# Gather sums in three steps, projection chunk by chunk: one change to a time-mix and mixture-of-experts kernel

## Time and profile before

| | us |
|---|---|
| median of 3 runs | 392.32 |
| the profiled execution | 395.08 |
| its span | 393.3 |
| PE busy | 322.4 (82% of the span) |
| DVE busy | 269.1 (68%) |
| POOL busy | 207.5 (53%) |
| ACT busy | 158.8 (40%) |
| projection matmuls L623 | 95.7, 744 instructions |
| all four periods, first pair to last product | 97.7 to 356.5 |
| tail: last projection, 16 gathers, sums, stores | 356.5 to 393.3 |

### The profile page before, as it was taken

One profiled execution on the slowest core, in us unless ns is written; L12 is line 12 of the kernel. 1 busy time (PEld: TensorE's weight loads), 2 busy tenths in 40 slices (PEclk: granted clock), 3 DMA queues, 4 the chain that ended last, 5 costly groups with the idle time before them and its releaser, 6 DMA issues.

```text
span 393.3 us, 6787 instructions
## 1 busy us (share of the span) xinstructions
PE 322.4 (82%) x2171; PEld 273.4 (70%) x2171; DVE 269.1 (68%) x846; ACT 158.8 (40%) x292; POOL 207.5 (53%) x241
## 2 busy tenths in 40 slices
PE   6976966855999999999999999999999897895000
PEld 3433553433987978999798899989999797885000
DVE  6598968385884987879868778795456774752235
ACT  2625421121654464555546454445554543452000
POOL 4536853887015563324646566727766668200674
PEclk9999766899999999999999999899999998999555
DMA  7863166104003112311112161123172133121112
GB/s 222 233 58 106 55 205 177 48 31 133 18 21 99 36 49 76 110 34 50 43 33 60 39 181 54 50 59 103 61 187 82 48 94 76 45 59 33 40 47 73
DMA packets 53058, 31.73 MB, mean 81 GB/s; under 512 B 12704, under 2 KB 48807, under 8 KB 53024
## 3 DMA queue, kind: packets, MB, share of 16 engines
q1 hardware_dynamic: 47840, 22.99, 21.2%
q0 software_dynamic: 4096, 8.06, 7.3%
q10 hardware_dynamic: 1088, 0.26, 0.3%
HBM read 18.92 MB, written 12.71 MB: 80 GB/s over the span
## 4 chain that ended last, share of the span: by engine, by line
PE 53%; DVE 15%; issue 11%; POOL 10%; DMA 6%; ACT 3%; POOLq 0%; SPq 0%; DVEq 0%; ACTq 0%
PE ps_o L623 16%; POOL picked L1146 4%; POOL slot_rows L1116 3%; DMA picked<-expert_rows,row_from 3%; PE pair0g L609 2%; PE bank L490 2%; PE bank L500 2%; PE bank L498 2%; PE pair1g L609 2%; PE pair0g L611 2%; PE pair0g L610 2%; PE bank L588 2%; DVE prod L1011 2%; PE pair0h L609 2%; PE pair0h L611 2%
## 5 line engine op out<-in xcount | busy, mean ns | idle before, releaser
L623 PE MATMUL ps_o<-proj_sb,hidden 128*104 128x128 f32 x744 | 95.7, 277 | 2.1 <-DVE o_sb L1020 2.1
L1146 POOL DMA_INDIRECT picked<-expert_rows,row_from x64 | 66.2, 1035 | 53.6 <-DVE prod L1011 18.6
L1116 POOL DMA_INDIRECT slot_rows<-x_ln,row_to x64 | 71.7, 1120 | 42.9 <-DVE prod L1011 24.4
L623 PEld LDWEIGHTS ps_o<-proj_sb,hidden 128*104 128x104 f32 x744 | 89.0, 172 | 4.1 <-issue 2.5
L748 ACT ACTIVATE gate_s<-pair0g,bgate_sb 128x308 f32<-128x308 f32 x64 | 33.1, 517 | 82.5 <-PE pair0g L611 82.5
L1011 DVE SCALAR_TENSOR_TENSOR prod<-pair1h,bfc_sb,gate_s 128x308 f32<-128x308 f32 x64 | 33.9, 530 | 24.1 <-ACT gate_s L748 22.6
L1011 DVE SCALAR_TENSOR_TENSOR prod<-pair0h,bfc_sb,gate_s 128x308 f32<-128x308 f32 x64 | 34.0, 532 | 22.6 <-ACT gate_s L748 20.6
L755 ACT ACTIVATE hidden<-prod 128x616 f32<-128x616 f32 x64 | 45.5, 711 | 8.6 <-DVE prod L1011 8.6
L748 ACT ACTIVATE gate_s<-pair1g,bgate_sb 128x308 f32<-128x308 f32 x64 | 32.9, 514 | 21.1 <-PE pair1g L611 20.6
L609 PE MATMUL pair1g<-slotT_hi,gate_hi 128*128 128x308 f32 x64 | 26.4, 413 | 4.4 <-DVE prod L1011 4.4
L609 PE MATMUL pair0g<-slotT_hi,gate_hi 128*128 128x308 f32 x64 | 26.0, 406 | 0.9 <-DVE prod L1011 0.5
(11 more groups left out here) (154 smaller groups left out, 727.1 us busy)
## 6 DMA issues: line engine op xcount, KB each, us to landing
slot_x<-slot_rows SPq DMA_DIRECT2D x20, 256.0 KB, 3.6
expert_rows<-o_sb SPq DMA_DIRECT2D x32, 156.0 KB
x_in<-in_L_attn_h SPq DMA_DIRECT2D x4, 512.0 KB, 5.3
prod<-in_L_ffn_w_gate SPq DMA_DIRECT2D x8, 256.0 KB, 2.7
prod<-in_L_ffn_w_c_fc SPq DMA_DIRECT2D x8, 256.0 KB, 3.0
proj_sb<-in_L_ffn_w_c_proj SPq DMA_DIRECT2D x8, 256.0 KB, 6.5
out<-picked SPq DMA_DIRECT2D x16, 128.0 KB, 2.1
slot_rows<-slot_x SPq DMA_DIRECT2D x5, 256.0 KB, 4.1
```

The lines of the kernel that those rows point to most:

```text
L623: mm = nc.tensor.matmul(ps_o[0:PART, P * part:P * part + P], hidden[:, e % 2, c, PART * part:PART * part + PART], proj_sb[:, e, c, :], sta ...
L1116: nc.gpsimd.indirect_dma_start(out=slot_rows, out_offset=bass.IndirectOffsetOnAxis(ap=row_to[:, c:c + 1], axis=0), in_=x_ln[:, b % RING, c ...
L1146: nc.gpsimd.indirect_dma_start(out=picked[:, j, k, :], out_offset=None, in_=expert_rows[b % 2], in_offset=bass.IndirectOffsetOnAxis(ap=row ...
```

## The change

Three things are changed; what is computed is not.

**1. The sum in three stages.** `gather_sum` is cut into `first_sum` (the wait for the gathers and the first multiply-adds), `second_sum`, and `sum_stats` (both statistics steps). Each has its own point:

| quarter (batches behind) | before: sum, rstd on POOL, norm | after: first, second, stats, rstd on POOL, norm |
|---|---|---|
| (2, q1), from period 2 on | 29, 29, 31 of the period before | 29, 30, 31 of the period before, then 0, 1 |
| (2, q2) | 3, 3, 6 | 1, 2, 3, 4, 6 |
| (2, q3) | 7, 7, 9 | 6, 7, 8, 9, 11 |
| (1, q0) | 10, 10, 13 | 10, 11, 12, 13, 15 |
| last period (1, q1) | 14, 14, 17 | 14, 15, 17, 18, 20 |
| last period (1, q2) | 18, 18, 21 | 18, 19, 21, 22, 24 |
| last period (1, q3) | 22, 22, 25 | 22, 23, 25, 26, 28 |

**2. Projection by chunk.** A piece is one matmul: chunk c, part; 12 pieces with the chunk outermost. Four pieces go to each of j = 1, 2, 3, in all periods.

**3. Its waits.** Chunks 0 and 1 wait only for the first silu of the expert, chunks 2 and 3 for the second. `project_last` is dropped; `project` over all 12 pieces does the same.

```diff
-PROJECTIONS = ({1: (0,), 2: (1,), 3: (2,)}, {2: (0,), 3: (1, 2)})
+PIECES = {j: tuple(range(4 * (j - 1), 4 * j)) for j in (1, 2, 3)}
...
-POOL_COMBINE = {10: [(1, 0)], 29: [(1, 1)], 3: [(2, 2)], 7: [(2, 3)]}
+POOL_COMBINE = {0: [(2, 1)], 4: [(2, 2)], 9: [(2, 3)], 13: [(1, 0)]}
...
-            def project(b, e, part):
+            def project(b, e, pieces):
+                for piece in pieces:
+                    c, part = divmod(piece, PARTS)
+                    if piece == 0:
+                        pe.wait_ge(hidden_made, nth(b, 2 * E, 2 * e + 1))
+                        if e or later(b):
+                            pe.wait_ge(o_copied, nth(b, E, e))
+                        else:
+                            pe.wait_ge(proj_in, 16 * E)
+                            pe.wait_ge(x_added, step(1, 3))
+                    if piece == 2 * PARTS:
+                        pe.wait_ge(hidden_made, nth(b, 2 * E, 2 * e + 2))
                     mm = nc.tensor.matmul(ps_o[0:PART, P * part:P * part + P],
                                           hidden[:, e % 2, c, PART * part:PART * part + PART], proj_sb[:, e, c, :],
-                                          start=(c == 0), stop=(c == HC - 1))
+                                          start=(piece == 0), stop=(c == HC - 1), skip_group_check=True)
...
                     if e > 0:
-                        for part in PROJECTIONS[b + 2 < B].get(j, ()):
-                            project(b, e - 1, part)
+                        project(b, e - 1, PIECES.get(j, ()))
...
-            def gather_sum(b, q):
+            def first_sum(b, q):
                 dve.wait_ge(gathered[q], nth(b, 16 * K * QT, 16 * K * QT))
...
                 i.then_inc(part_made, 1)
+
+            def second_sum(b, q):
+
                 dve.wait_ge(part_made, nth(b, QUARTERS, q + 1))
...
                 i.then_inc(y_made, 1)
+
+            def sum_stats(b, q):
+
                 dve.wait_ge(y_made, nth(b, QUARTERS, q + 1))
```

More of the change, by code:

```diff
@@ L110 @@
 VECTOR_ROUTE = {0: [("norm", 4)], 1: [("norm", 5)], 4: [("top", 0)], 5: [("top", 1), ("choice", 0)], 8: [("rows", 0)]}
[L112 to L118, removed]
+VECTOR_COMBINE = {1: [("final_norm", 2, 1), ("first_sum", 2, 2)], 2: [("second_sum", 2, 2)], 3: [("sum_stats", 2, 2)],
+                  6: [("final_norm", 2, 2), ("first_sum", 2, 3)], 7: [("second_sum", 2, 3)],
+                  8: [("sum_stats", 2, 3)], 10: [("first_sum", 1, 0)],
+                  11: [("final_norm", 2, 3), ("second_sum", 1, 0)], 12: [("sum_stats", 1, 0)],
+                  15: [("final_norm", 1, 0)], 29: [("first_sum", 1, 1)], 30: [("second_sum", 1, 1)],
+                  31: [("sum_stats", 1, 1)]}
+VECTOR_COMBINE_LAST = {1: [("final_norm", 2, 1), ("first_sum", 2, 2)], 2: [("second_sum", 2, 2)], 3: [("sum_stats", 2, 2)],
+                       6: [("final_norm", 2, 2), ("first_sum", 2, 3)], 7: [("second_sum", 2, 3)],
+                       8: [("sum_stats", 2, 3)], 10: [("first_sum", 1, 0)],
+                       11: [("final_norm", 2, 3), ("second_sum", 1, 0)], 12: [("sum_stats", 1, 0)],
+                       14: [("first_sum", 1, 1)], 15: [("final_norm", 1, 0), ("second_sum", 1, 1)],
+                       17: [("sum_stats", 1, 1)], 18: [("first_sum", 1, 2)], 19: [("second_sum", 1, 2)],
+                       20: [("final_norm", 1, 1)], 21: [("sum_stats", 1, 2)], 22: [("first_sum", 1, 3)],
+                       23: [("second_sum", 1, 3)], 24: [("final_norm", 1, 2)], 25: [("sum_stats", 1, 3)],
+                       28: [("final_norm", 1, 3)]}
 POOL_MIX = {15: [("rstd", 2)], 17: [("rstd", 3)], 26: [("rstd", 4)], 31: [("rstd", 5)]}
@@ L126 @@
 GATHERS_LAST = {**{p: (2, 12 + p) for p in range(0, 4)}, **{p: (1, p - 4) for p in range(4, 20)}}
-POOL_COMBINE = {10: [(1, 0)], 29: [(1, 1)], 3: [(2, 2)], 7: [(2, 3)]}
-POOL_COMBINE_LAST = {3: [(2, 2)], 7: [(2, 3)], 10: [(1, 0)], 14: [(1, 1)], 18: [(1, 2)], 22: [(1, 3)]}
+POOL_COMBINE = {0: [(2, 1)], 4: [(2, 2)], 9: [(2, 3)], 13: [(1, 0)]}
+POOL_COMBINE_LAST = {0: [(2, 1)], 4: [(2, 2)], 9: [(2, 3)], 13: [(1, 0)], 18: [(1, 1)], 22: [(1, 2)], 26: [(1, 3)]}
 OUT_STORES = {0: [(2, 1), (2, 2)], 1: [(2, 3)], 2: [(1, 0)]}
 OUT_STORES_LAST = {0: [(2, 1), (2, 2)], 1: [(2, 3)], 2: [(1, 0)], 3: [(1, 1)], 4: [(1, 2)], 5: [(1, 3)]}
-PROJECTIONS = ({1: (0,), 2: (1,), 3: (2,)}, {2: (0,), 3: (1, 2)})
+PIECES = {j: tuple(range(4 * (j - 1), 4 * j)) for j in (1, 2, 3)}
 SLOT_TURNS = {6: (0, 3), 18: (0, 4), 28: (1, 0), 29: (1, 1), 30: (1, 2)}
@@ L642, in period @@
+                    if piece == HC * PARTS - 1:
+                        mm.then_inc(o_made, 1)
             def period(b):
@@ L649, in period @@
                     if e > 0:
-                        for part in PROJECTIONS[b + 2 < B].get(j, ()):
-                            project(b, e - 1, part)
+                        project(b, e - 1, PIECES.get(j, ()))
                     if point == 1 and b > 0:
-                        for part in range(PARTS):
-                            project(b - 1, E - 1, part)
+                        project(b - 1, E - 1, range(HC * PARTS))
                     if point in SLOT_TURNS:
@@ L674, in _ @@
                 period(b)
-            project_last()
+            project(B - 1, E - 1, range(HC * PARTS))
         @block.scalar
@@ L991, in gather_sum @@
                 i.then_inc(y_moments_made, 1)
+            def gather_sum(b, q):
+                first_sum(b, q)
+                second_sum(b, q)
+                sum_stats(b, q)
             def final_norm(b, q):
@@ L999, in final_norm @@
                 i.then_inc(y_normed, 1)
-            combine_stages = {"gather_sum": gather_sum, "final_norm": final_norm}
+            combine_stages = {"first_sum": first_sum, "second_sum": second_sum, "sum_stats": sum_stats, "final_norm": final_norm}
             def product(b, e, j):
```

## The result

The changed kernel took 394.32 us, the median of 21 runs, against 392.56 us for the kernel before in as many. The ratio is 1.0036, 95% interval 1.0022 to 1.0050: slower by 0.36%. The ratio leaves out one of the 21, a slow one of 401.58 us. I had forecast 382.5 us.

What follows compares the result with a forecast made beforehand. PE was taken to bound all four periods, idling 8.3 us. Terms: -2.1 (periods 0 and 1), -1.5 (period 2), -5.2 (period 3), -1.0 (clock) = -9.8, from a median of 392.32 to 382.5 us; range 379.5 to 389.5.

Steps and rivals of the forecast that it cites:

- Its points: Periods 0 and 1: projection pieces moved to j = 1 and 2 cover PE's waits there, -2.1 us.
- The sum in three stages: Period 3: less of the sum stands ahead of products and copy-out on DVE, and POOL waits less for statistics: -5.2 us.
- Period 2 and the wait at point 28: Period 2: lighter sums gain, but PE newly waits about 1 us for slot rows at point 28: -1.5 us, bounds 0 and -2.5.
- The chain: Period 2: copy-out of point 8, store, gather, 16 scatters, slot load; said to have no slack and to grow 1.0 us.
- my sign that the chain was not binding: Point 28 of period 2: absence of the forecast PE wait for slot rows, about 1 us, would show this.
- The clock: Period 3: the half-clock stretch behind the stall of point 14 costs 1.7 us, of which 1.0 goes: -1.0 us.
- Order and half waits: Projection chunk by chunk: 0, bounds -2.5 and +1 us; waits on the silu halves: 0 to -0.5, counted as 0.1.
- The base: The 9.8 us gain, set against the profiled execution of 395.08 us, was taken off the median of 392.32: 382.5 us.
- R3: Point 1 of periods 2 and 3: DVE meets waits for rstd and gather, PE stands behind: +2.6, 394.9 us; chance 0.09.
- R1: Periods 2 and 3: transfers (gathers, scatter chain) set the pace, so only work ahead of them counts: 387.2 us; chance 0.23.

Runs made afterwards that it cites:

- e1: Kernel before with only the new projection pieces (four at each of j = 1, 2, 3, chunk outermost), sums whole: 398.31 us, ratio 1.0141.
- e7: Kernel before with chunk order and half waits only, pieces at the old places, sums whole: 393.12 us, ratio 1.0009.
- e8: Kernel before, unchanged, run again for a second trace and a measure of noise: 393.10 us, ratio 1.0016.
- e5: Changed kernel with SP storing quarter (2, q1) ahead of the store of expert 0: 390.49 us, ratio 0.9936.
- e6: Changed kernel, pieces of periods 0 and 1 back at j = 2 and 3, and (2, q1) stored ahead of expert 0: 383.96 us, ratio 0.9783.
- e4: Changed kernel with the final norm of (2, q3) moved from point 11 to point 13: 394.45 us, ratio 1.0046.
- e9: Kernel before with the sums in three stages and (2, q1) stored ahead of expert 0, projection untouched: ratio 0.9761.
- e11: Repeat of the changed kernel with the pieces of periods 0 and 1 back at j = 2 and 3, on another chip: ratio 0.9842.
- e10: Kernel before with only the store of (2, q1) put ahead of the store of expert 0: ratio 0.9918.
- e3: Changed kernel with pieces of periods 0 and 1 back at j = 2 (four) and j = 3 (eight), chunk order kept: 389.42 us, ratio 0.9915.

## Why the prediction was wrong, step by step

**Its points (-2.1, bounds -2.4 to +0.5): this step failed.** It came to +6.35 us (3.04 + 3.31), 8.45 us off, most of the miss. I priced what the pieces at j = 1 would cover, and tested only the products on the other side. The first piece has a second wait, `o_copied`, and its releaser stands on DVE behind the mix. In the profile of before nothing waited there, since the first part stood a point later; the wait has no row, and I should have taken DVE's rows of points 11, 15, 23 and 27 and asked when the copy-out ends. In its place PE waited 3.2 and 4.0 us for the copy-out. e1 and e7 show it: 5.2 us for the places alone, with whole sums. The small waits of the earlier trace rows did go.

**The sum in three stages (-5.2 in period 3).** The mechanism was right: late products and POOL's waits for statistics went. Point 7 came back whole, and of the late products of points 14 to 22 no more than 0.3 us is left. But a term is missing from the sum: I let POOL's rstd of q3 move behind the gather of point 8 and counted only its 1.0 us in the scatters. The norm at point 11 waits for it: 2.0 and 2.1 us of PE in periods 2 and 3. Period 3 gave 4.5 us (58.88 to 54.41), where this term and the clock's together had 6.2; of the 4.5, 1.5 to 2.0 is the slow stretch (1.5 by e8's period 3, 2.0 by PE's busy time). With the store out of the way (e5) it gives 7.7 from rows 2, 6.2 from e8.

**Period 2 and the wait at point 28 (-1.5).** The period gave 1.6, and that it is so near is luck: it came from the clock, while PE's waits grew. The chain did grow, from 28.5 us (258.93 to 287.42) between copy-out and slot load to 29.9 (262.62 to 292.52). PE did not wait at point 28, my sign that the chain was not binding; it had lost 2.0 us at point 13. Whether the chain would bind without that was not tried by itself. In e6, where that wait is gone and the store goes out early, it takes 28.4 us (256.61 to 285.04) and PE waits for no slot rows.

**The clock (-1.0).** Both slow stretches are gone from the changed kernel's trace, and PE's busy time in periods 2 and 3 with them is 2.7 and 2.0 us less. That is more than I took, but e1, e7 and e8 have none, two and one of them, and e4, the changed kernel but for one norm, has the second (clock 0.97 in period 3). I treated one execution's stretches as the kernel's; how often they come in the runs that were only timed is not shown, and neither is what they are worth in the median.

**Order and half waits (0 and -0.1).** Right (e7).

**The base.** I took a gain worked out against one execution and subtracted it from a median 2.8 us lower. By e8 the second slow stretch, 1.5 us of it, was part of the gain I counted. It does not explain all of the 2.8 us, as e7 has it too and lies on its median; e7's first pair starts at 96.5 us, that of rows 2 at 97.7.

**The rivals.** R3 had the right kind (DVE meets a wait ahead of what PE needs) at the wrong place: at point 1 of periods 2 and 3 DVE waited 0.60 and 0.84 us for the rstd, and no wait of PE is listed there. That its 394.9 us is near the 394.3 measured is luck. R1's gathers were indeed in the way, and what held them was a store.

## What to carry to other kernels

When work is moved to an earlier point, list every wait of its first instruction, and read for each releaser what stands before it on its own engine at that point; a wait that the old place never met has no row in the profile. When a wait only moves as its stage is moved (e4), follow the late engine back to where it first stood still, and mistrust the releaser that the row names if it had long been done. Work out a gain from two traces of the kernel before, not from one.

## What the runs showed of the hardware that I had not expected

On the chip of e9 to e11 the kernel before is 10 us slower (403.4 against 392.8). In e11's trace ACT stands still for 4 us at point 18 of period 2, with nothing of this core's program named as its releaser (the row says "remote"), and DVE with it; period 2 is 63.08 us there, against 57.8 in the changed kernel on the first chip:

```profile
278.86 0.60 ACT L729 ACTIVATE slotT_hi<-bank 128x512 fp32r<-128x512 f32 x1 [4.01 <-remote]
...
279.49 0.69 DVE L883 TENSOR_TENSOR slotT_lo<-bank,slotT_hi 128x512 fp32r<-128x512 f32 x1 [4.49 <-ACT slotT_hi L729]
```

e9's trace has the same wait of DVE at the same point (4.52 us). Waits ended by "remote" stand in all three traces of that chip (in e10 the longest is 2.3 us, of DVE) and in none of the nine usable traces of the others, and so do waits of ACT before its gate copies that end with no releaser at all (12.2 us in seven in e11, 10.1 in six in e9). Periods 0 and 1 are as long there as elsewhere. The cause stays open. The ratios on that chip are those of the others within the intervals (e11 0.9842 for e3's 0.9915, e9 0.9761 for e6's 0.9783).
